# LayerNorm variance of the self-attention tasks from accumulated row sums and squares, and the q and k projections in two slots

## What is computed

```python
def _layernorm(x, axis=-1, eps=1e-05):
    m = jnp.mean(x, axis=axis, keepdims=True)
    v = jnp.var(x, axis=axis, keepdims=True)
    return (x - m) / jnp.sqrt(v + eps)

def _L0_attn_ref(x, wq, bq, wk, bk, wv, bv, wo, bo):
    q = jnp.einsum('bsd,hde->bhse', x, wq) + bq
    k = jnp.einsum('bsd,hde->bhse', x, wk) + bk
    v = jnp.einsum('bsd,hde->bhse', x, wv) + bv
    scores = jax.nn.softmax(jnp.einsum('bhse,bhte->bhst', q, k) * scale, axis=-1)
    att = jnp.einsum('bhst,bhte->bhse', scores, v)
    ...
    return att @ wo.T + bo

x = _layernorm(x + _L0_attn_ref(x, ...), axis=-1)
x = _layernorm(x + _L0_xattn_ref(ctx_1024, x, ctx_1024, ...), axis=-1)
x = _layernorm(x + _L0_ffn_ref(x, ...), axis=-1)
```

## Time and profile before

| | us |
|---|---|
| median of 3 runs | 369.61 (368.77 to 369.62) |
| profiled execution | 368.67 |
| its span on the core | 366.9 |
| busy: DVE / PE / ACT / POOL | 328.6 / 267.3 / 255.5 / 189.1 |
| one period of four slots, mean of 8 | 15.33 |

### The profile page before, as it was taken

The page is one execution under the profiler, slowest core; times in us unless marked ns, Lnnn a source line. Parts: engine busy times, 40 slices in busy tenths (PEclk is TensorE's granted clock), DMA queues, the critical chain, the costliest instruction groups (busy, mean ns, idle before and its releaser), DMA issues.

```text
span 366.9 us, 13218 instructions
## 1 busy us (share of the span) xinstructions
PE 267.3 (73%) x4899; PEld 170.7 (47%) x4899; DVE 328.6 (90%) x718; ACT 255.5 (70%) x504; POOL 189.1 (52%) x382
## 2 busy tenths in 40 slices
PE   3669878998888988889888898888783466102960
PEld 2446545565655655656565565555452121001540
DVE  5657798899999999999999999999989599998994
ACT  2126877687878878788787888778672499605965
POOL 5244778566665665656666566665222005400385
PEclk9999999899999999999999999999997586755995
DMA  1352332324233233232332324332000000000024
GB/s 50 99 153 67 85 90 61 89 76 113 75 91 104 75 98 96 76 97 82 105 98 70 95 76 118 84 90 79 15 5 1 0 0 0 0 0 3 0 88 143
DMA packets 48998, 25.19 MB, mean 69 GB/s; under 512 B 6440, under 2 KB 48808, under 8 KB 48936
## 3 DMA queue, kind: packets, MB, share of 16 engines
q1 hardware_dynamic: 48216, 24.02, 22.9%
q10 hardware_dynamic: 720, 0.33, 0.3%
HBM read 9.39 MB, written 2.10 MB: 31 GB/s over the span
## 4 chain that ended last, share of the span: by engine, by line
DVE 40%; PE 17%; issue 17%; POOL 12%; SPq 6%; DMA 4%; ACT 3%; DVEq 0%; POOLq 0%; ACTq 0%
DVE neg_max L787 15%; DVE h_ext L893 5%; DVE h_ext L894 5%; PE ps L1019 4%; PE ps L1045 4%; SPq L351 4%; PE ps L1061 3%; POOL rstd L489 2%; DVE arena_q L929 2%; ACT probs L622 2%; DVE r_sum L797 2%; DMA arena_h<-parts_cq 2%; POOL o_root L556 2%; DVE arena_q L804 1%; PE ps L1087 1%
## 5 line engine op out<-in xcount | busy, mean ns | idle before, releaser
L787 DVE TENSOR_REDUCE neg_max<-ps 128x8 f32<-128x1024 f32 x128 | 155.7, 1217 | 13.2 <-PE ps L1019 11.8
L611 ACT ACTIVATE probs<-ps 128x1024 f32<-128x1024 f32 x64 | 65.6, 1024 | 19.8 <-PE ps L1026 18.6
L1019 PE MATMUL ps<-arena_h 31*128 31x128 f16 x1024 | 52.8, 222 | 35.0 <-DVE neg_max L787 22.9
L622 ACT ACTIVATE probs<-ps 128x1024 f32<-128x1024 f32 x64 | 65.6, 1025 | 17.6 <-PE ps L1026 16.1
L1019 PEld LDWEIGHTS ps<-arena_h 31*128 31x128 f16 x1024 | 30.9, 94 | 67.8 <-DVE neg_max L787 40.2
L486 POOL TENSOR_TENSOR var_eps<-mean_var,eps_col 128x1 f32<-128x1 f32 x64 | 12.2, 191 | 81.6 <-DVE mean_var L834 81.6
L1026 PE MATMUL ps<-arena_h 32*128 32x128 f16 x1024 | 51.6, 219 | 0.5 <-ACT probs L611 0.5
L1045 PE MATMUL ps<-probs,arena_q 128*32 128x128 f32 x1024 | 42.2, 284 | 0.9 <-issue 0.9
L1045 PE MATMUL ps<-probs,arena_h 128*32 128x128 f32 x1024 | 41.2, 279 | 0.2 <-ACT probs L611 0.2
L489 POOL TENSOR_TENSOR rstd<-var_eps,minus_half 128x1 f32<-128x1 f32 x64 | 35.2, 550 | 5.2 <-PE ps L1045 0.2
L1026 PEld LDWEIGHTS ps<-arena_h 32*128 32x128 f16 x1024 | 29.5, 93 | 1.5 <-issue 0.9
(11 more groups left out here) (152 smaller groups left out, 641.2 us busy)
## 6 DMA issues: line engine op xcount, KB each, us to landing
arena_h<-parts_sq SPq DMA_DIRECT2D x48, 64.0 KB, 1.9
arena_h<-parts_ck SPq DMA_DIRECT2D x48, 64.0 KB, 2.0
arena_h<-parts_cq SPq DMA_DIRECT2D x48, 64.0 KB, 2.1
arena_h<-parts_sk SPq DMA_DIRECT2D x45, 64.0 KB, 2.0
xT_in<-in_xT_dram SPq DMA_DIRECT2D x16, 128.0 KB, 2.3
xN_in<-in_xN_dram SPq DMA_DIRECT2D x16, 128.0 KB, 2.2
cT_in<-in_cT_dram SPq DMA_DIRECT2D x16, 128.0 KB, 2.5
cN_in<-in_cN_dram SPq DMA_DIRECT2D x16, 128.0 KB, 2.4
```

Of the source, the lines that this page charges most:

```text
L611: act.activation(probs[1][:, :], ps_s2, ACT.Exp, scale=SCALE).then_inc(ex, 1)
L622: act.activation(probs[0][:, :], ps_s2, ACT.Exp, scale=SCALE).then_inc(ex, 1)
L787: dve.tensor_reduce(neg_max[b.par][:, HH * half:HH * half + HH], ps_s1.rearrange("p (h k) -> p h k", h=HH), AXX, ALU.max, negate=True).the ...
L1019: ins = pe.matmul(ps_s1[:, at:at + S], q[r:r + MAX_AT, j, :], kk[r:r + MAX_AT, j, :], start=True, stop=True, skip_group_check=True)
```

## The change

For S tasks only, `bn_stats` and `bn_aggr` go. The residual is added by a `scalar_tensor_tensor` that also writes the sum of each row (`y_sum`). POOL multiplies it by -1/128 (`y_shift`). ACT squares `y + y_shift` and accumulates the row sum of the squares (`y_sq`). POOL turns that into `var_eps` and `rstd` as before. DVE's normalisation of an S task moves from the middle of the slot to its end, the transpose on PE and the copy on ACT one slot later. The wait of POOL for the squares stands behind the splits of `sk` and `cq`, and ahead of `x_bias` and of the splits of `sq` and `ck`. Apart from that, q of an S pair is projected, and taken out of PSUM, one slot before k (`Q_AT` = 6), in the plain slot, except for the five pairs of the lead; the load of its input (`XT_AT`) comes one slot earlier. C tasks keep `bn_stats` and `bn_aggr`.

```diff
-XT_AT, XN_AT, CT_AT, CN_AT = 7, 3, 8, 6
+XT_AT, XN_AT, CT_AT, CN_AT = 8, 3, 8, 6
+Q_AT = 6
...
+def k_pair(k):
+
+    return S_FIRST.get(k + QK_AT)
+
+
+def q_pair(k):
+
+    i = S_FIRST.get(k + Q_AT)
+    if i is not None and i >= LEAD_PAIRS:
+        return i
+    i = S_FIRST.get(k + QK_AT)
+    return i if i is not None and i < LEAD_PAIRS else None
...
             def slot(k):
                 v = task(k - 4)
-                if v is not None:
-
-                    pool.wait_ge(ag, v.pos + 1)
-                    pool.tensor_tensor(var_eps[v.par][:, :], mean_var[v.par][:, 1:2], eps_col[:, :], ALU.add).then_inc(ve, 1)
+
+                def root():
                     pool.wait_ge(ve, v.pos + 1)
                     need(pool, xn, v.pos - 1)
                     pool.tensor_tensor(rstd[v.par][:, :], var_eps[v.par][:, :], minus_half[:, :], ALU.pow).then_inc(rq, 1)
+
+                if v is not None and v.kind == "C":
+
+                    pool.wait_ge(ag, v.m + 1)
+                    pool.tensor_tensor(var_eps[v.par][:, :], mean_var[v.par][:, 1:2], eps_col[:, :], ALU.add).then_inc(ve, 1)
+                    root()
+                if v is not None and v.kind == "S":
+                    pool.wait_ge(yy, v.pos + 1)
+                    pool.tensor_tensor(y_shift[v.par][:, :], y_sum[v.par][:, :], minus_mean[:, :], ALU.mult).then_inc(sh, 1)
                 i = S_FIRST.get(k + FILL_AT)
                 if i:
                     pool.wait_ge(eqk, 2 * i + 2)
...
 
                     pool.wait_ge(txe, 2 * i + 2)
                     split(pool, "cq", cq_full[i % RING][:, :], i)
+                if v is not None and v.kind == "S":
+                    pool.wait_ge(sq, v.m + 1)
+                    pool.tensor_scalar(var_eps[v.par][:, :], y_sq[v.par][:, :], 1.0 / D, EPS, ALU.mult, ALU.add).then_inc(ve, 1)
+                    root()
                 i = S_FIRST.get(k + BIAS_AT)
...
                     act.mul(max_rows[nxt.par][:, :], ps_x[0:H, S:2 * S], 1.0 / MROW).then_inc(mte, 1)
+                if v is not None and v.kind == "S":
+                    act.wait_ge(sh, v.m + 1)
+                    act.activation(square[v.par][:, :], y_sb[v.par][:, :], ACT.Square, bias=y_shift[v.par][:, :],
+                                   accum_out=y_sq[v.par][:, :]).then_inc(sq, 1)
                 if k >= LEAD_SLOTS:
                     evacuations()
...
-                if v is not None and v.kind == "S":
-                    act.wait_ge(tx, v.m + 1)
-                    need(act, split_done["cq"], v.pair - RING + 1)
-                    act.copy(cq_full[v.ring][:, v.half * S:v.half * S + S], ps_x[:, 2 * S:3 * S]).then_inc(txe, 1)
+                if t is not None and t.kind == "S":
+                    act.wait_ge(tx, t.m + 1)
+                    need(act, split_done["cq"], t.pair - RING + 1)
+                    act.copy(cq_full[t.ring][:, t.half * S:t.half * S + S], ps_x[:, 2 * S:3 * S]).then_inc(txe, 1)
...
-                if x is not None:
+                if x is not None and x.kind == "S":
                     dve.wait_ge(oo, x.pos + 1)
-                    if x.kind == "S":
-                        dve.wait_ge(xb, x.pair + 1)
-                        dst, own, residual = y_sb[x.par][:, :], ps_o[:, 0:D], x_bias[x.ring][:, x.half, :]
-                    else:
-                        dve.wait_ge(xn, S_POS[x.m] + 1)
-                        dst, own, residual = (by_group(y_sb[x.par][:, :]), by_group(ps_o[:, 0:D]),
-                                              in_groups(x1_all[:, x.m, :]))
-                    dve.tensor_tensor(dst, own, residual, ALU.add).then_inc(yy, 1)
+                    dve.wait_ge(xb, x.pair + 1)
+                    dve.scalar_tensor_tensor(out=y_sb[x.par][:, :], in0=ps_o[:, 0:D], scalar=1.0,
+                                             in1=x_bias[x.ring][:, x.half, :], op0=ALU.mult, op1=ALU.add,
+                                             accum_out=y_sum[x.par][:, :]).then_inc(yy, 1)
+                if v is not None and v.kind == "S":
+                    dve.wait_ge(rq, v.pos + 1)
+                    dve.tensor_scalar(in_groups(x1_all[:, v.m, :]), by_group(y_sb[v.par][:, :]), y_shift[v.par][:, :],
+                                      rstd[v.par][:, :], ALU.add, ALU.mult).then_inc(xn, 1)
```

More of the change, by code:

```diff
@@ L195, in decoder_layer @@
         mean_var = [sb(f"mean_var{i}", [128, 2]) for i in range(2)]
+        y_sum, y_sq = [sb(f"y_sum{i}", [128, 1]) for i in range(2)], [sb(f"y_sq{i}", [128, 1]) for i in range(2)]
+        y_shift, square = [sb(f"y_shift{i}", [128, 1]) for i in range(2)], [sb(f"square{i}", [128, D]) for i in range(2)]
         var_eps = [sb(f"var_eps{i}", [128, 1]) for i in range(2)]
@@ L568, in slot @@
             def slot(k):
[L569 removed]
+                a, z, w, v, t, nxt = task(k), task(k - 1), task(k - 2), task(k - 4), task(k - 5), task(k + 1)
                 def evacuations():
[L571 to L576 removed]
+                    for j, (i, full, name) in enumerate(((q_pair(k), q_full, "sq"), (k_pair(k), k_full, "sk"))):
+                        if i is not None:
+                            if i == 0 and j == 0:
+                                act.wait_ge(b_ready, 1)
+                            act.wait_ge(pqk, 2 * i + 2 if q_pair(k) == k_pair(k) else 2 * i + 1 + j)
                             need(act, split_done[name], i)
@@ L1112, in slot @@
                     need(pe, yy, x.pos)
-                    for first, at, n, each in ((S_FIRST, QK_AT, eqk, 2), (S_FIRST, V_AT, evv, 1), (C_FIRST, CK_AT, eck, 1)):
+                    if k_pair(k) is not None:
+                        pe.wait_ge(eqk, 2 * k_pair(k) + 2)
+                    elif q_pair(k) is not None:
+                        pe.wait_ge(eqk, 2 * q_pair(k) + 1)
+                    for first, at, n in ((S_FIRST, V_AT, evv), (C_FIRST, CK_AT, eck)):
                         i = first.get(k + at)
                         if i is not None:
-                            pe.wait_ge(n, each * (i + 1))
+                            pe.wait_ge(n, i + 1)
                     pe.matmul(ps_o[:, 0:D], attT[:, :], (wo_self if x.kind == "S" else wo_cross)[:, :],
```

67 lines of the change are left out of this document (34 added, 33 removed).

## The result

| | before | after |
|---|---|---|
| median, us | 369.19 (367.32 to 369.62) | 375.50 (375.07 to 378.82) |
| profiled execution / its span | 368.67 / 366.9 | 375.61 / 373.7 |
| busy DVE / ACT / POOL | 328.6 / 255.5 / 189.1 | 322.4 / 266.7 / 193.8 |
| period of four slots, mean of nine | 15.31 | 15.52 |
| the same, without any wait for `cq` | 15.11 | 15.26 |

A forecast was written before the change was run, and what follows sets the result against it. DVE, busy 90% of the span, was taken as the bound. Periods of 15.26 against 15.33 won 0.8 us and the lead lost 0.7, giving 368.6 profiled and a median of 369.5 us; range 365.0 to 374.2.

The forecast's parts named there:

- The lead: First slots: 0.7 us lost, between -0.8 and +2.5, the upper end with a second clock dip of PE, about 1.2 us.
- What waits for it: POOL's variance, behind ACT's squares, starts 1.47 us later; `ck` split, fills and `cq` landing follow; period 15.26 against 15.33.
- the plain slot's middle: DVE's half-slot with the added q projection and evacuation: 1.73 us plus 0.02, so 1.75.
- the CK slot's end: S normalisation added to the C task's three DVE operations: 1.95 + 0.25 = 2.20 us, bounds +0.17 to +0.47.
- the term for the QK slot's end: One q projection and evacuation leave the chain, so this half-slot falls from 2.00 to 1.73 us.
- the first limit: PE's scores and DVE's maximum share PSUM banks, so a half-slot takes at least about 1.73 us.
- The forecast limit of 14.82: DVE's own limit for a period of four slots, down from 15.16 us, 0.34 less.
- the QK slot's middle: DVE's first half-slot of the QK slot, left at 2.05 us in the sum of DVE's limit.
- the landing chain: POOL, SP, DMA to `parts_cq`: 14.4 us a period with short landings (DVE's 14.82 holds), 15.7 with long; half and half.
- Rival 2: Chain through POOL and SP bounds every period, from the `ck` split behind the squares: 15.75 a period, 374.8 us; chance 0.17.

The follow-up runs named there:

- no_sq_wait: Changed kernel, but POOL's S variance reads a ready tile with factor 0 instead of waiting for ACT's squares (output differs); 368.86 us, ratio 1.000.
- xbias_first: Changed kernel with `x_bias` moved ahead of POOL's wait for the squares; 373.54 us, ratio 1.012.
- pool_late: Kernel before, with 1.85 us of fills on POOL in 14 CK slots, between variance root and `x_bias`; 386.77 us, ratio 1.049.
- early_turn: On top of both_orders, PE's transpose and ACT's copy to `cq_full` in mid-slot in slots 6 and 58; 372.18 us, ratio 1.009.
- cq_late: Kernel before, with 1.1 us of fills on POOL ahead of the `cq` split, 16 times; 374.09 us, ratio 1.013.
- q_alone: Kernel before, with only q projected one slot ahead of k and its input loaded a slot earlier; 367.11 us, ratio 0.996.
- both_orders: Changed kernel with `x_bias` ahead of POOL's wait for squares and the S root ahead of the same slot's `cq` split; 374.00 us, ratio 1.014.

## Why the prediction was wrong

Point by point, by the prediction's own steps.

**Right.** The work itself was sized well. The accumulator read on DVE took 0.08 us (I took 0.13) and the residual 0.28. ACT's square took 0.38, as said, and its accumulator read 0.19 (I took 0.2). POOL started the S variance at C + 1.68 (forecast C + 1.63; C is 191.31), ended the `ck` split at C + 4.52 (4.55), SP began the `ck` fill at C + 4.59 (4.62), and the third `cq` transfer at C + 8.3 (8.4). The V slot took 1.79 and 1.72 (1.73, 1.75), the CK slot 1.77 and 2.17 (1.73, 2.20). The lead lost 1.0 us up to slot 13 (0.7), with a stop of DVE of 2.83 in slot 6 (2.4). Waits for `parts_cq` grew from 5.3 to 11.0.

**Wrong, step "What waits for it".** I followed POOL's delay to the `ck` split, SP and the landing, and stopped there. The C task's root stands in the same queue, behind the `ck` split, and DVE needs it in the plain slot's middle. I had the order in the listing of the change and the times to work it out: `ck` split until C + 4.55, variance and root 0.8 more, so C + 5.35, against a DVE that gets there at C + 1.73 + 2.20 + 1.3 = C + 5.23. I gave the plain slot's middle 1.75. It was 2.14, 0.39 more, in eight of nine periods (1.97 in the ninth, behind the long half-slot of 3.07). By these times the late root alone would cost 0.12. The rest is the overlap that I had wrong: a normalisation that starts as the root ends runs under the `cq` split, and is held for its length. I had the two lengths 0.25 and 0.47 for just that, and used them at the CK slot's end alone. The runs show it by three ways: no_sq_wait (1.76), xbias_first (1.77) and pool_late (2.78).

**Wrong, the term for the QK slot's end.** 1.73 was forecast for a half-slot that only PSUM limits, and it took 1.90. The maximum ends at 202.37, PE's scores start at 202.62, 0.25 later and not 0.06. The 0.06 came from the earlier trace rows, in the middle of a slot. In after, where no landing is waited for, the gap is 0.05 to 0.11 in the middles, 0.05 or 0.06 ahead of the CK and QK slots, and never under 0.25 ahead of the V and plain slots. Those two begin with a new pair, and there the code has PE wait on two more semaphores, for the operand stacks, even when the stacks landed long ago; that these waits are the reason is likely, but no run takes them out. The trace of before has the same 0.25 and more in the same places. So the first limit is about 1.73 at one place and up to 1.9 at another. The forecast limit of 14.82 would be 14.99 with it. That xbias_first ran at 14.86 all the same is because the QK slot's middle, forecast at 2.05, took 1.91 there: two errors that cancel.

**Wrong, the tail.** I looked for the moved copy to `cq_full` in the lead (slot 6) and not at the other end of `ORDER`, where slot 58 has the same pattern. It cost 2.1 us, the largest single item, about half of it with PE's clock. early_turn shows it.

**Right in kind, wrong in size: the landing chain.** I had every other period at 15.7. In cq_late, six of eleven are at 15.6 or more, so how often it strikes was about right; but three of them are 2 us above that, because PE's clock fell, for which I had a term in the lead alone. In after itself the chain mostly lay under the late root: of nine periods, two were above 15.6 by `cq` (15.62 and 16.27) and one by `sk` (16.00). cq_late showed what the chain costs without that cover.

**The sum by what the runs showed.** Slots 13 to 57: undisturbed +0.15 x 11 = 1.7 and disturbed ones 1.5 more; lead 1.0, tail 2.1, the rest 0.5: 6.8 us of span. The forecast had 0.8 won, 0.7 lost. Rival 2 gave 374.8, near the result, but with its price put on the landing in every period. The wait that it named, POOL behind the squares, was the cause; the place where it bit first was another.

**Why thinner work on DVE gave nothing.** no_sq_wait has DVE's shorter work and no delay on POOL. Beside q_alone, with the full `bn_stats`, its undisturbed periods are no shorter, 14.98 against 14.92. Its V slot is 0.15 shorter (3.52 against 3.67). Its QK slot is the same (3.81), since that slot's end stands at the 1.90 that PE's scores allow in both. Its CK slot is 0.25 longer (4.03 against 3.78), since the normalisation now stands at the slot's end on top of the C task's residual and `bn_stats`. The forecast had that last term, at 0.25. The means, 14.92 and 15.05, differ by 0.13, and the medians say the opposite, 368.86 and 367.11, with the long tail in the first. No run puts the CK slot's normalisation elsewhere, so what the thinner work would be worth in a better place is open.

## What to carry to other kernels

When an operation on an in-order engine gets a later input, list everything behind it in that queue and ask for each when its reader needs it, not only for the one at the end of the longest chain. Small work that others don't wait for belongs ahead of such a wait: moving one 0.7 us instruction gave back 0.4 us of every period here. Ask also what the late work will then run beside. Look for an irregular order's exceptions at both of its ends, and give an idle stretch of some 2 us on PE a second price: in some of these traces the clock fell behind it, and the fall cost as much again.

## What the runs showed of the hardware that I had not expected

- **DVE held by POOL.** The normalisation of 128x128 (SBUF to SBUF) takes 0.25 us alone, 0.47 beside `x_bias` (q_alone, 187.17) and 0.63 under the `cq` split (after, 196.64), each time until just behind that one's end. Order on POOL alone moved its mean from 403 to 300 ns for S tasks.
- **Accumulators are cheap.** DVE's read 0.08 us; ACT's 0.19. On DVE the next instruction began in the same moment as the read (190.93).
- **PE's clock after a wait.** After 1.88 us without work in PE (both_orders, 167.33) it stood at half for about 3 us, which doubled the price of the wait; after 2.12 us in the same execution (229.85) it stayed full.
- **PE's start behind a maximum.** 0.05 to 0.07 us after it ahead of the CK and QK slots, and never under 0.25 ahead of the V and plain slots, in before and after alike.
- **Landing of 64 KB between SBUF places.** From 1.9 to 4.0 us, mostly 1.9, for the same transfer; and three issues on SP's queue took from 1.83 to 3.38 us.
